# Loads of the keys' stacks moved from SyncE's queue to GpSimd's

## What is computed

```python
# L2 (queries, keys over C ** 0.5 and a temperature, the diagonal masked)
attn = einsum('bhnd,bhmd->bhnm', q, k) / C ** 0.5 / temperature
attn = softmax(where(diag, -inf, attn));  out = einsum('bhnm,bhmd->bhnd', attn, v)
# L3 (causal)
scores = einsum('bhqd,bhkd->bhqk', q, k) * HEAD_SIZE ** -0.5
weights = softmax(where(causal, scores, -inf));  out = weights @ v
...
t = t + L2_attn(ln(t));  t = t + L2_ffn(ln(t));  t = t + L3_attn(ln(t));  t = t + L3_ffn(ln(t))
```

## Time and profile before

| | us |
|---|---|
| median of 3 runs | 917.91 (914.95 to 918.13) |
| profiled execution, own time | 918.22 |
| its span, first to last instruction | 916.5 |
| granted clock of PE, mean share of full speed | 0.948 |
| attention of L2 / experts of L2 | about 277 to 415 / 415 to 595 |
| attention of L3 / experts of L3 | about 596 to 732 / 732 to 916 |

### The profile page before, as it was taken

How to read it: one execution, slowest core, us unless ns; L and a number is a source line. 1 busy time by engine, 2 the same in 40 slices (tenths; PEclk the granted TensorE clock), 3 DMA queues, 4 the chain that set the end, 5 groups by cost and what they waited for, 6 DMA issues and landing times.

```text
span 916.5 us, 18605 instructions
## 1 busy us (share of the span) xinstructions
PE 792.8 (86%) x6130; PEld 656.2 (72%) x6130; DVE 548.3 (60%) x1632; ACT 487.9 (53%) x777; POOL 320.2 (35%) x365
## 2 busy tenths in 40 slices
PE   1898996899447999889999999789888799999997
PEld 1666664889325677667999998666666688888886
DVE  4799994553626688884555655445777644444442
ACT  0366665111324877775555655447777655555553
POOL 2211112910131444354333344514553553333332
PEclk9999995899758999999999999959999999999999
DMA  4750000000034554510000000344646000000000
GB/s 87 131 101 8 0 0 1 1 0 0 1 79 102 111 112 90 109 22 1 1 1 0 0 0 9 80 94 100 120 92 123 8 1 10 9 9 9 9 9 18
DMA packets 27570, 38.01 MB, mean 41 GB/s; under 512 B 9288, under 2 KB 24352, under 8 KB 27424
## 3 DMA queue, kind: packets, MB, share of 16 engines
q1 hardware_dynamic: 27520, 37.36, 19.7%
HBM read 25.06 MB, written 12.29 MB: 41 GB/s over the span
## 4 chain that ended last, share of the span: by engine, by line
PE 51%; ACT 8%; DVE 5%; DMA 4%; issue 3%; POOL 1%; SPq 1%; ACTq 0%; DVEq 0%; POOLq 0%
PE ps L1331 18%; PE ps L1323 13%; DMA keys<-at_parts 3%; PE ps L1148 3%; PE ps L1170 3%; PE ps L1186 3%; PE ps L1163 2%; ACT at_qs L1456 2%; DVE at_mf L1605 2%; ACT at_pT L1452 2%; PE ps L1213 2%; PE ps L1165 1%; PE ps L1310 1%; PE ps L1192 1%; SPq L1018 1%
## 5 line engine op out<-in xcount | busy, mean ns | idle before, releaser
L1516 ACT ACTIVATE ff_h<-ps,b 128x512 f32<-128x512 f32 x192 | 128.6, 687 | 116.2 <-PE ps L1323 115.8
L1331 PE MATMUL ps<-w,ff_h 128*128 128x96 f32 x1536 | 181.9, 275 | 6.7 <-ACT ff_fT L1522 6.7
L1331 PEld LDWEIGHTS ps<-w,ff_h 128*128 128x128 f32 x1536 | 178.5, 192 | 11.3 <-issue 8.4
L1720 DVE SCALAR_TENSOR_TENSOR tok<-ps,ff_gate,tok 128x96 f32 (+1 forms) x224 | 56.0, 311 | 121.1 <-PE ps L1331 117.0
L1605 DVE TENSOR_REDUCE at_mf<-ps 128x4 f32<-128x1024 f32 (+2 forms) x96 | 100.3, 1081 | 28.1 <-PE ps L1165 27.9
L1058 POOL TENSOR_SCALAR_AFFINE_SELECT at_pT<-at_pT 128x768 f32<-128x768 f32 x64 | 65.8, 1030 | 146.0 <-ACT at_pT L1452 145.4
L1452 ACT ACTIVATE at_pT<-ps 128x1024 f32<-128x1024 f32 (+2 forms) x96 | 87.0, 917 | 22.8 <-PE ps L1170 20.3
L618 DVE SCALAR_TENSOR_TENSOR ca_qk<-ps,dw,ca_qk 96x225 f32<-96x225 f32 (+1 forms) x256 | 97.6, 447 | 2.0 <-ACT ca_qk L467 2.0
L1163 PE MATMUL ps<-keys,at_qs 96*128 96x256 bf16 (+1 forms) x384 | 73.2, 276 | 29.4 <-DMA keys<-at_parts 19.8
L1323 PE MATMUL ps<-ff_xh,ff_wh 96*128 96x512 f32 x192 | 79.7, 415 | 1.3 <-DVE tok L1626 0.9
L1323 PE MATMUL ps<-ff_xh,ff_wl 96*128 96x512 f32 x192 | 75.4, 393 | 0.0
(11 more groups left out here) (231 smaller groups left out, 1529.9 us busy)
## 6 DMA issues: line engine op xcount, KB each, us to landing
at_parts<-at_part SPq DMA_DIRECT2D x96, 96.0 KB
at_qs<-at_parts SPq DMA_DIRECT2D x16, 288.0 KB, 4.3
keys<-at_parts SPq DMA_DIRECT2D x16, 288.0 KB, 5.3
at_qs<-at_parts SPq DMA_DIRECT2D x16, 192.0 KB, 5.8
keys<-at_parts SPq DMA_DIRECT2D x16, 192.0 KB, 6.2
w<-in_L_ffn_w SPq DMA_DIRECT2D x4, 576.0 KB
chan<-in_x SPq DMA_DIRECT2D x4, 384.0 KB, 5.5
at_qs<-at_parts SPq DMA_DIRECT2D x16, 96.0 KB, 6.5
```

The source lines that it names most:

```text
L1331: ins = nc.tensor.matmul(ps[:, 6 + e % 2, C * t:C * (t + 1)], h[:, e % 2, j, P * t:P * (t + 1)], L.f.w2[:, e * HC + j, :], start=(j == 0), ...
L1516: nc.scalar.activation(h[:, e % 2, j, :], ps[:, 3 * (e % 2) + j, :], ACT.Gelu, bias=L.f.b1[:, e * HC + j:e * HC + j + 1]).then_inc(f_h, 1)
```

## The change

The three loads of the keys' stack of a pair leave SP's `stacks` and become `stack_keys`, run by POOL on its own DMA queue, with semaphores of their own (`s_keys`, one for each slot). SP keeps all stores and the three loads of the queries. PE's body waits for both semaphores, each with half the former count. `stack_keys(i)` waits for the stores of pair `i` (`s_part`); it has no wait of its own for the slot, since on POOL it stands behind the masks of pair i-2, which follow the exps of all its transposed scores.

Where it stands on POOL: for pairs 0 and 1 behind `normed(2)`, ahead of the attention of L2; in the bodies between the second masks of `i-1` and `normed(i+3)`, for pair `i+1`; for pair 8 at the end of part 6 of the experts of L2; for pair 9 in part 7, behind `normed(9)` and ahead of `normed(10)`. The loop over bodies is written two at a time, so that the slot is known.

```diff
--- before.py
+++ after.py
@@ -880,6 +880,7 @@
          "out_normed", "out_turned", "outT", "proj", "tok", "stats", "mv", "rstd", "parts_stored"))
     s_rstd_in, s_zero = sem("at_rstd_in"), sem("at_masked")
     s_stack = [sem(f"at_stacks{k}") for k in range(2)]
+    s_keys = [sem(f"at_keys{k}") for k in range(2)]
     s_own_dve = sem("at_dve_own")
     (f_ones, f_xn, f_own, f_T, f_xT, f_xh, f_xl, f_w, f_gt, f_nm, f_ex, f_gd, f_own_pool, f_bt, f_tb, f_F, f_h, f_Y, f_ac,
      f_st, f_mv, f_OT, f_oc, f_store) = (sem(f"ff_{n}") for n in (
@@ -1013,11 +1014,9 @@
 
                         sp.wait_ge(s_ST, 6 * i - 6)
                     for row, count in ((0, 3), (3, 2), (5, 1)):
-                        for t, stack in enumerate((qs, ks)):
-                            start = 3 - count if t else 0
-                            sp.dma_start(stack[D * row:D * (row + count), slot, :, :, :].rearrange("r h u n -> r (h u n)"),
-                                         L.parts_d[t, start:start + count, :, bass.ds(i - L.first, 1), :, :].rearrange(
-                                             "k d i h n -> (k d) (i h n)")).then_inc(s_stack[slot], 16)
+                        sp.dma_start(qs[D * row:D * (row + count), slot, :, :, :].rearrange("r h u n -> r (h u n)"),
+                                     L.parts_d[0, 0:count, :, bass.ds(i - L.first, 1), :, :].rearrange(
+                                         "k d i h n -> (k d) (i h n)")).then_inc(s_stack[slot], 16)
 
                 stacks(L2, 0, 0, False)
                 stacks(L2, 1, 1, False)
@@ -1058,6 +1057,13 @@
                         pool.affine_select(out=block, in_=block, compare_op=ALU.is_ge if L.causal else ALU.not_equal, fill=0.0,
                                            base=0, pattern=[[0, H], [1, P]], channel_multiplier=-1).then_inc(s_zero, 1)
 
+                def stack_keys(L, i, slot):
+                    pool.wait_ge(s_part, 96 * i + 96)
+                    for row, count in ((0, 3), (3, 2), (5, 1)):
+                        pool.dma_start(ks[D * row:D * (row + count), slot, :, :, :].rearrange("r h u n -> r (h u n)"),
+                                       L.parts_d[1, 3 - count:3, :, bass.ds(i - L.first, 1), :, :].rearrange(
+                                           "k d i h n -> (k d) (i h n)")).then_inc(s_keys[slot], 16)
+
                 def weights_low(L):
                     pool.wait_ge(f_w, 1 + 2 * L.last)
                     if L.last:
@@ -1087,9 +1093,12 @@
                         elif e:
                             link(pool.tensor_tensor(bias[:, :, :], bias[:, :, :], term[:, :, :], ALU.add))
 
-                def body(L, i, back, ahead, gates):
+                def body(L, i, slot, back, ahead, fetch, gates):
                     if back:
                         masked(L, i - 1, 1)
+                    if fetch:
+
+                        stack_keys(L, i + 1, 1 - slot)
                     if ahead:
                         normed(L, i + 3)
                     masked(L, i, 0)
@@ -1102,12 +1111,15 @@
 
                 def attention(L):
                     first, end = L.first, L.end
-                    body(L, first, 0, True, 0)
-                    body(L, first + 1, 1, True, 0)
-                    with pool.Fori(first + 2, end - 3) as i:
-                        body(L, i, 2, True, 0)
-                    for i in range(end - 3, end):
-                        body(L, i, 2, False, i - (end - 3))
+                    body(L, first, 0, 0, True, False, 0)
+                    body(L, first + 1, 1, 1, True, True, 0)
+                    with pool.Fori(first // 2 + 1, first // 2 + 2) as j:
+                        body(L, 2 * j, 0, 2, True, True, 0)
+                        body(L, 2 * j + 1, 1, 2, True, True, 0)
+                    body(L, end - 4, 0, 2, True, True, 0)
+                    body(L, end - 3, 1, 2, False, True, 0)
+                    body(L, end - 2, 0, 2, False, True, 1)
+                    body(L, end - 1, 1, 2, False, False, 2)
                     masked(L, end - 1, 1)
                     token_rstd(m, pool, end - 2 - first, end - 2, s_rstd, s_mv)
                     biases(L, first)
@@ -1119,9 +1131,13 @@
                     if ahead:
                         low(i + 1)
                         biases(L, i + 1)
+                    if pair is not None:
+                        stack_keys(L3, pair, pair % 2)
 
                 for i in range(3):
                     normed(L2, i)
+                for i in range(2):
+                    stack_keys(L2, i, i)
                 attention(L2)
                 part_(L2, 0, True, None)
                 parts(part_, L2, pool)
@@ -1216,7 +1232,8 @@
 
                 def body(L, i, slot, back, ahead, nxt, gates):
 
-                    pe.wait_ge(s_stack[slot], 48 * (i - slot) + 96)
+                    pe.wait_ge(s_stack[slot], 24 * (i - slot) + 48)
+                    pe.wait_ge(s_keys[slot], 24 * (i - slot) + 48)
                     if back:
                         pe.wait_ge(s_ex, 6 * i - 3)
                     else:
```

## The result

| | before | after |
|---|---|---|
| median, us | 917.64 (914.95 to 918.13) | 932.37 (931.71 to 932.84) |
| profiled execution, own time | 918.22 | 932.84 |
| its span | 916.5 | 931.1 |
| granted clock of PE, mean | 0.948 | 0.936 |

The change makes the kernel slower: 1.0158 times the time of before, 95% interval 1.0124 to 1.0193. The forecast was 941.5 with a range of 927 to 960.

What follows compares the result with a forecast made beforehand. PE, busy 86%, was taken to bound the kernel through when it stands still. 918.2 + 19.1 (entry of L3) + 4.5 (loops) = 941.8, or 941.5 against the median; range 927 to 960.

Steps and rivals of the forecast that it cites:

- The mechanism of the entry: Entry of L3: two waits for stores on in-order POOL delay normalizations 9 and 10 and PE's turns: +19.1 us.
- Issue on POOL: Each keys' load issue on POOL takes 1.0 us, near one pass of that engine; 3.0 us a pair.
- Normalization behind the issues: Entry of L3: after each wait and its three issues, POOL normalizes the next pair in 3.74 us.
- Clock: Entry of L3: PE's stand puts part of the following 8.5 us of its work at 1.2 GHz: 2.5 us.
- The loops: Keys land 0.6 us later: 3.6 us over six L3 pairs, about 0.9 over six L2 pairs; +4.5 us together.
- the end of the batch stays where it is: Loop: keys issued later on POOL don't delay the batch's end, as queries' 576 KB still need over 2 us.
- Rival 1: Loops: last key load lands 7.3 us after issue even on its own queue; 18 us, not 4.5; 955; chance 0.16.
- Rival 2: Issues cost 0.35 us, loops unmoved; entry gives back 4.0 us, undisturbed clock 2.5 more: 931; chance 0.12.
- Rival 3: VectorE stretches POOL's issues to 1.9 us each; entry 5.4 us more, loops 16 us: 959; chance 0.08.
- Rival 4: Faster: overlapping queues land keys early everywhere and both waits at L3's entry are covered: 910; chance 0.04.
- The cover of 4.4 us against 3.0: Loop: POOL's 2.91 us idle before the masks plus 1.5 behind them hide 3.0 us of issues: no cost.
- The entry of L2: POOL's waits for stores of pairs 0 and 1 are hidden by its 17.66 us idle there: 0.

Runs made afterwards that it cites:

- A: Changed kernel with POOL's normalizations of pairs 9 and 10 issued ahead of both waits for stores: 912.5 us, 0.9944 of before; again 912.2, 0.9934.
- B: Changed kernel keeping only the first wait: keys of pair 8 ahead of normalization 9, but normalization 10 ahead of keys of 9: 924.8 us, 1.0080 of before.
- C: Changed kernel keeping only the second wait: normalization 9 ahead of keys of 8, but keys of 9 ahead of normalization 10: 921.7 us, 1.0045 of before.
- D: Changed kernel with 80 unused transposes of the identity on PE ahead of the turn of pair 9: 930.0 us, 1.0149 of before.
- E: Kernel before, all six loads on SyncE's one queue, three of the queries then three of the keys: 916.7 us, 0.9982; again 915.0, 0.9972.
- H: Kernel before, loads still alternating queries and keys, sizes rotated so neighbours never write the same partitions: 915.2 us, 0.9963 of before.
- I: A with each load of the keys split in two by heads, six issues a pair on POOL instead of three: 919.5 us, 0.9995 of before.
- G: Kernel before with the keys read from the queries' plane of the stored parts, order unchanged: 918.2 us, 1.0008 of before.
- J: A with POOL's three loads of the keys in the order 192, 96, 288 KB: 916.2 us, 0.9972 of before.

## Why the prediction was right, and where its sizes were not

*The mechanism of the entry: right, and shown.* Both waits stand where they were forecast, both turns are released by POOL, and kernels A, B and C take them away and give them back one by one. The forecast was +19.1 us for the entry against a measured +17.2. In the profile before everything that was needed could be read: the normalization of 9 was done before the stores of 8 landed, and that of 10 long before those of 9. The prediction puts both ahead of the stores of 8, which is not exact: 586.88 is 0.28 us after 586.60. Nothing in its sum hangs on that. The total lies inside the range of 927 to 960, but 932.4 is just below the 933 to 948 that the forecast gave to its own mechanism; a part of being right is the width of the range.

*The terms of that sum.* After leads by 1.6 us when it issues the first load of pair 8 (585.13 against 586.76). Counted from there, the turn of pair 9 came 8.8 us late (10.2 forecast), the low parts of pair 9 12.3 (12.7), the turn of pair 10 17.7 (19.7).
- Issue on POOL: 1.0 us was taken, 0.54 measured (0.49 to 0.77), twice three of them: -2.8 us. The step that failed is the one in which an issue was priced by a pass of the engine. It is nearer to SyncE's 0.35. The 48 issues (ns, shortest, median, longest); the first of three takes 0.61:

```profile
L1063 POOL DMA_DIRECT2D keys<-at_parts x48: 491/519/771, 266.0 to 722.4; - x48
```

- Normalization behind the issues: 3.74 taken, 3.48 to 3.49 measured (586.85 to 590.34): -0.5 in both.
- From the landing to the first issue on POOL: 0.27 measured (584.97 to 585.24). At the first wait 0 was taken; at the second about 0.16, since 600.25 is SyncE's first issue and not the landing: +0.4 in both.
- Clock: 2.5 taken, 3.5 measured: +1.0. D shows that it is the clock.

With these four put right, the turn of pair 10 is forecast 17.8 us late, against 17.7.

*The loops: wrong.* +4.5 us was forecast, 0.0 measured. The failed step is "the end of the batch stays where it is". It rested on 0.98 of DMA share at 147 GB/s, read as a limit of the engines; the share was right and the conclusion was not, for at the same share after moves 175 to 223 GB/s, and E and H on one queue 191 to 218 in 31 of 32 batches. (By its own rate of 147 GB/s, 1152 KB would take 8.0 us, not the 7 that it names.) A share of busy time says that the engines were occupied, not that they could do no more. In the loops the last part of the keys lands 0.7 to 1.5 us sooner after the first issue than in the same pair of before, and not 0.6 us later. The sooner landing brings nothing either: in the loop the wait before the scores was 0.27 us, and behind it the next thing late is an exp or VectorE's maxima, so the period stays at 16.1 us. The Trainium skill, "DMA: Bandwidth & Descriptors", section "Issuing engines are not separate DMA queues", says that loads of several issuers interleave on the same 16 engines and save only the sequencer's time. E agrees, as it reaches that rate on one queue; that the order of loads on one queue can change the rate by a third was in none of the forecast's steps.

*Rival 1* (landing follows the issue, 955) fell: in the loops the last load lands 4.8 to 5.4 us after its issue, not 7.3. *Rival 2* (cheap issues, 931) comes nearest in time, and its unmoved loops are what was measured; but the issues cost 0.54 and not 0.35, and its undisturbed clock wasn't there. That 931 is so near to 932.4 is in part luck. *Rival 3* (VectorE stretches POOL's issues) did not come about. In after 17 of the 48 issues have VectorE busy beside them, nine of these from end to end, and these nine take 0.49 to 0.59 us, no more than the others. In I the six issues from 657.69 to 660.78 have VectorE busy for 1.34 us beside them, and take 3.09 us, 0.52 each. But no issue of after stood beside the low parts, whose pass is the one that the rival named (L1614 here). The stretching to five times, which the Trainium skill describes in "SBUF — State Buffer", section "SBUF: two separate sides", is not seen: the longest of the 48 takes 0.77 us. Its example is a copy of VectorE's; the passes beside these issues read PSUM (`ps`), but for two copies of 0.08 us, so this case neither bears the page out nor speaks against it. *Rival 4* (faster) was right about its own condition: it needed the two waits covered, and with them out of the way, in A, the change is faster, by 5 us.

*The cover of 4.4 us against 3.0.* It was never tried at 3.0 in after, where the issues take 1.61. I tried it with 3.09: it holds in L2, and in L3 it costs 0.6 us a pair. So the 1.5 us of slack behind the masks, which were added to POOL's idle time, are not cover of the same kind; why not is open. It is not that a mask becomes longer: a couple takes 2.66 us in before, 2.67 in after, and in I at most that.

*The entry of L2: 0, right.* POOL waits there for 9.9 us and nobody waits for POOL; PE's stand for the keys is 11.19 us against 12.38. The stretch from the first load to that of pair 2 is 32.4 us against 32.0.

*The sum.* 918.2 + 19.1 + 4.5 = 941.8 against 932.8. Of the 9.0 us too many, 4.5 are the loops, 1.9 the entry, and 2.6 lie in stretches that the change doesn't touch or that no step spoke of.

## What to carry to other kernels

A wait put on an in-order engine is paid by what stands behind it: before a wait for a DMA is moved there, list what that engine issues next and who consumes it, and put that work ahead of the wait. The same loads cost 14.7 us in one place of POOL's program and gained 5 in another, of which some 3 can be had by their order alone. And a DMA share near 1 isn't a limit: look at the GB/s beside it, and try the order of the transfers before another queue.

## What was not expected of the hardware

Two loads of the same size to the same partitions, issued one behind the other on SyncE's queue, move 144 to 169 GB/s in the middle of a batch at a DMA share of about 1 (30 of the 32 batches of before and G; pair 7 has 184 in both). With neighbours of other sizes and partitions, the same 1152 KB move at 187 to 218 (47 of the 48 batches of E's two profiles and H's; one of E has 160), and the last landing comes about 1 us sooner. It did not hold for two queues started together (the entries of after, A and J).

How fast the clock came back after a short stand of PE at 592 to 596 differed widely for nearly the same work. After a stand of 4.25 us it was at 0.50 until about 618; in A, with 3.07 us, it was back at 1.00 by 608, but in E's second profile, with a stand of only 1.70 us, it was still at 0.50 from 608 to 612:

```profile
604.00:608.00 4.00, 3.48 (x18) 1.91 (x16) 1.88 (x2) 1.01 (x1) 2.06 (x3) 0.64 0.95 201
608.00:612.00 4.00, 3.06 (x37) 2.73 (x37) 3.50 (x6) 3.52 (x5) 1.26 (x1) 1.00 0.20 56
```

```profile
608.00:612.00 4.00, 3.44 (x24) 2.31 (x23) 2.95 (x3) 1.55 (x3) 0.00 (x0) 0.50 0.50 111
```

The first block is A's, the second E's. With it go 2.2 us of difference between two profiles of one kernel (33.3 and 31.1 in the two of E), and this is why the small gains above are read from medians. What sets the time of the return stays open.
